# First feed-forward of a four-stage fused block: the last six weight chunks rounded by VectorE alone, and three pieces of work put elsewhere in their engines' orders

## What is computed

```python
wq = w.astype(jnp.float8_e4m3fn).astype(x.dtype)
y = jnp.einsum('bsi,io->bso', x, wq)
return y * scale

gate = jax.nn.silu(_quantized_matmul(x, gate_w, gate_scale))
up = _quantized_matmul(x, up_w, up_scale)
return _quantized_matmul(gate * up, down_w, down_scale)
```

## Time and profile before

| | us |
|---|---|
| Median of 3 runs (723.23 to 723.35) | 723.33 |
| The profiled execution's own time | 722.73 |
| Its span, first to last instruction | 720.9 |
| PE busy / DVE busy | 660.1 / 548.9 |
| ACT busy / POOL busy | 479.7 / 436.0 |

### The profile page before, as it was taken

How to read it: one execution, slowest core, us unless ns; L and a number is a source line. 1 busy time by engine, 2 the same in 40 slices (tenths; PEclk the granted TensorE clock), 3 DMA queues, 4 the chain that set the end, 5 groups by cost and what they waited for, 6 DMA issues and landing times.

```text
span 720.9 us, 16231 instructions
## 1 busy us (share of the span) xinstructions
PE 660.1 (92%) x5782; PEld 527.8 (73%) x5782; DVE 548.9 (76%) x1180; ACT 479.7 (67%) x982; POOL 436.0 (60%) x618
## 2 busy tenths in 40 slices
PE   2789999988899999999999999999999999999784
PEld 1567777667788877888888888888888888876442
DVE  3699999999787877676777676676767766766887
ACT  1577877756466576666666666666666666658994
POOL 2378878878877545565656656665656554464500
PEclk9999999999999999999999999999999999999997
DMA  8200003203201000000000100000100000000001
GB/s 282 77 9 9 10 9 117 70 1 106 86 1 38 15 1 2 15 30 9 23 24 17 28 9 25 23 16 16 31 9 16 15 1 3 1 1 1 31 29 60
DMA packets 26019, 22.83 MB, mean 32 GB/s; under 512 B 5041, under 2 KB 24402, under 8 KB 25810
## 3 DMA queue, kind: packets, MB, share of 16 engines
q1 hardware_dynamic: 24160, 20.92, 9.2%
q10 hardware_dynamic: 1778, 0.86, 0.4%
HBM read 19.67 MB, written 2.10 MB: 30 GB/s over the span
## 4 chain that ended last, share of the span: by engine, by line
POOL 38%; issue 26%; PE 15%; DVE 14%; ACT 3%; ACTq 1%; POOLq 1%; DVEq 0%
POOL rstd L734 14%; POOL pr L702 5%; POOL p_n L709 5%; PE banks L1594 2%; POOL w L725 2%; POOL w_raw L722 2%; PE banks L1613 2%; PE banks L1614 2%; DVE h_sum L1093 2%; DVE hid_b L1086 2%; POOL var L732 1%; POOL qk_norm L644 1%; DVE h_magic_b L1091 1%; DVE half L852 1%; POOL hid_lo L671 1%
## 5 line engine op out<-in xcount | busy, mean ns | idle before, releaser
L734 POOL TENSOR_TENSOR rstd<-var,minus_half 128x8 f32<-128x8 f32 x64 | 106.1, 1657 | 5.0
L709 POOL TENSOR_TENSOR p_n<-pr,pinv 128x256 f32<-128x256 f32 x64 | 39.3, 614 | 75.7 <-DVE pinv L1001 75.7
L702 POOL TENSOR_TENSOR pr<-pr,rstd 128x256 f32<-128x256 f32 x63 | 38.6, 613 | 74.1 <-DVE pr L1011 74.0
L1316 ACT ACTIVATE kT<-banks,gk_q 128x512 f32<-128x512 f32 x64 | 44.0, 688 | 49.1 <-PE banks L1755 49.1
L1745 PE MATMUL banks<-m_hi,z_hi 128*128 128x256 f32 x256 | 74.9, 293 | 0.7 <-DVE z_lo L992 0.6
L1745 PE MATMUL banks<-m_hi,z_lo 128*128 128x256 f32 x256 | 72.3, 283 | 0.0
L1745 PE MATMUL banks<-m_lo,z_hi 128*128 128x256 f32 x256 | 72.3, 282 | 0.0
L992 DVE TENSOR_TENSOR z_lo<-banks,z_hi 128x512 fp32r<-128x512 f32 x64 | 43.9, 686 | 29.1 <-ACT z_hi L1301 29.0
L1039 DVE TENSOR_REDUCE sums<-q_sq 128x4 f32<-128x512 f32 x64 | 43.7, 683 | 25.2 <-ACT q_sq L1340 25.2
L1362 ACT ACTIVATE qT<-banks 128x512 f32<-128x512 f32 x64 | 38.2, 597 | 32.9 <-PE banks L1849 32.9
L1007 DVE TENSOR_REDUCE pmax<-banks 128x4 f32<-128x256 f32 x64 | 27.0, 422 | 41.1 <-PE banks L1776 41.0
(11 more groups left out here) (194 smaller groups left out, 2059.2 us busy)
## 6 DMA issues: line engine op xcount, KB each, us to landing
w_raw<-in_L_xattn_Wq SPq DMA_DIRECT2D x4, 512.0 KB, 5.8
wo_raw<-in_L_xattn_Wo SPq DMA_DIRECT2D x1, 2048.0 KB, 9.2
k_ctx<-in_ctx SPq DMA_DIRECT2D x16, 128.0 KB, 2.7
w_raw<-in_L_ffn_w_gating SPq DMA_DIRECT2D x16, 128.0 KB, 2.3
out_x<-x_sb SPq DMA_DIRECT2D x4, 512.0 KB, 2.9
x_sb<-in_x SPq DMA_DIRECT2D x1, 1536.0 KB, 9.3
a_ctx<-in_ctx SPq DMA_DIRECT2D x16, 64.0 KB, 1.8
w_raw<-in_L_xattn_Wk SPq DMA_DIRECT2D x2, 512.0 KB, 9.1
```

The lines of the kernel that those rows point to most:

```text
L702: pool.tensor_tensor(pr[:, u % 2, :, :], pr[:, u % 2, :, :], roots_of[:, HC:2 * HC].unsqueeze(2).to_broadcast([P, HC, S]), ALU.mult).then_ ...
L709: pool.tensor_tensor(p_n[:, u % 2, :, :], pr[:, u % 2, :, :], pinv[:, u % 2, :].unsqueeze(2).to_broadcast([P, HC, S]), ALU.mult).then_inc( ...
L734: pool.tensor_tensor(rstd1[:, par, :], var1[:, :], minus_half[:, :].to_broadcast([P, 2 * HC]), ALU.pow).then_inc(root1, 1)
L1316: act.activation(kT[u % 2][:, :, :].rearrange("p h n -> p (h n)"), bank[2][:, :], ACT.Copy, scale=gk_q[:, :]).then_inc(kT_ready, 1)
```

## The change

The first late chunk is now chunk 12 instead of chunk 13. A new function rounds a chunk wholly on VectorE, and it stands where the late chunks' `w0_magic` stood, one place later each: chunk 12 after `rows_updated(NT - 2)`, chunk 13 in the step u = 2, and so on to chunk 17 in the step u = 6. GpSimd rounds chunks 0 to 11 only. On VectorE the four `normal` of tiles 4 to 7 move from between `hidden(0)` and `hidden(1)` to the step u = 2, behind `rows_updated(NT - 1)` and ahead of chunk 13, and `rows_updated(NT - 2)` now stands ahead of chunk 12's rounding. On GpSimd `weights_lo(23)` comes behind `hidden_lo(23)`.

```diff
-W0_LATE = W0_CHUNKS - 5
+W0_LATE = W0_CHUNKS - 6
...
+        def w0_rounded_here(dve, n):
+
+            w0_magic(dve, n)
+            dve.wait_ge(magic_steps, 2 * n + 2)
+            dve.wait_ge(w0_steps, 2 * n)
+            dve.tensor_tensor(w0_raw[:, w0_part(n)], w0_raw[:, w0_part(n)], rnd[:, n % 2, :], ALU.add).then_inc(w0_steps, 1)
+            dve.wait_ge(w0_steps, 2 * n + 1)
+            dve.tensor_tensor(w0[:, w0_part(n)], w0_raw[:, w0_part(n)], rnd[:, n % 2, :], ALU.subtract).then_inc(w0_steps, 1)
...
             probabilities0(NT - 1)
-            w0_rounded(pool, 12)
             rows_biased(NT - 1)
             hidden_lo(0)
             weights_lo(0)
             hidden_lo(1)
-            w0_rounded(pool, W0_LATE)
             weights_lo(1)
...
-                weights_lo(u)
+                if u < NG * J0 - 1:
+                    weights_lo(u)
                 hidden_lo(u)
-                if u <= W0_CHUNKS - W0_LATE:
-                    w0_rounded(pool, W0_LATE + u - 1)
             run_groups(J0, step, 2)
+            weights_lo(NG * J0 - 1)
...
             w0_magic(dve, 11)
-            w0_magic(dve, 12)
             exponential_sums0(NT - 1)
             hidden(0)
-            for r in range(GT, 2 * GT):
-                normal(r, f_xhat, f_xhat_ready, fT_done)
             hidden(1)
-            w0_magic(dve, W0_LATE)
             rows_updated(NT - 2)
+            w0_rounded_here(dve, W0_LATE)
...
                 hidden(u)
                 if u == 2:
                     rows_updated(NT - 1)
+                    for r in range(GT, 2 * GT):
+                        normal(r, f_xhat, f_xhat_ready, fT_done)
...
                 if u <= W0_CHUNKS - W0_LATE:
-                    w0_magic(dve, W0_LATE + u - 1)
+                    w0_rounded_here(dve, W0_LATE + u - 1)
```

## The result

The changed kernel takes 728.08 us (727.32 to 728.71, 6 runs), the kernel before 723.34 (722.45 to 725.38, 6 runs): a ratio of 1.0066 (95% interval 1.0054 to 1.0078), 4.7 us slower. The forecast was 2.5 us slower, 725.8 with a range up to 728.0. The direction and the places were right, the size was not. The two profiled executions lie further apart than the medians: 728.71 us, the slowest of its six, against 722.73.

What follows compares the result with a forecast made beforehand. TensorE was taken to bound the stage, except at its start, where group 0's down products wait for GpSimd's rounding. Profiled 722.73 + 3.2 (later products) - 0.7 (stage end) = 725.2, median 0.6 higher: 725.8 us, range 724.3 to 728.0.

Steps and rivals of the forecast that it cites:

- The replay: Group 0, chunk by chunk: 6.7 us of new TensorE waiting less 3.5 removed, chunk 17's product 3.2 us later.
- the two holds behind the long waits: GpSimd low halves hold chunk 13's second magic step (to 177.41) and chunk 17's subtraction (to 193.8).
- The tail: Stage end: the last low half no longer stands behind 0.74 us of next-stage weights, -0.7 us.
- the term for the clock: Rival, 20%: TensorE's clock halves after standing still 175.6 to 178.4, costing 0.8 to 1.7 us; a second fall up to 728.5.
- The rival that the holds fall away: Group 0: VectorE mostly not held by GpSimd, chunk 17's product 0.36 us earlier than before, time 722.2, no change; 11%.
- the last subtraction: Chunk 17: if only this VectorE instruction escapes GpSimd's low half, its product starts at 192.9, time 724.7.
- GpSimd's relief: Rival, 4%: VectorE delivers every chunk by its due time, all 3.5 us and the 0.7 come back: 719.1.

Runs made afterwards that it cites:

- both waits filled: The changed kernel with 11 unread matmuls before the second down product and 8 before chunk 17's, in TensorE's two long waits: 725.37 us, ratio 1.0034.
- the mended version: The changed kernel with normalisations of tiles 4 to 7 back, chunk 17 right behind hidden(6), those of tiles 8 to 11 behind group_scaled(0): 721.48 us, ratio 0.9970.
- chunk 13 first: The changed kernel with chunk 13 rounded ahead of the four normalisations in the step u = 2: 726.69 us, ratio 1.0053.
- chunk 17 first: The changed kernel with chunk 17 rounded ahead of the four normalisations of tiles 8 to 11 in the step u = 6: 726.0 us, ratio 1.0047.
- the first filled: The changed kernel with 11 unread matmuls in TensorE's first long wait only, ahead of the second down product: 726.1 us, ratio 1.0039.

## Why the prediction was wrong

- **The replay held.** Product 1 was forecast at 178.45 - 173.96 = 4.49 us after product 0: 4.47. Product 5, at 193.94 - 173.96 = 19.98: 20.07 with the clock kept up. The releasers were the ones named, and the two holds behind the long waits too: magic step at chunk 13, subtraction at chunk 17, with the 0.15 and about 0.3 us behind GpSimd's end that the earlier trace rows gave. At chunk 16 the replay held both magic steps. The rows of the kernel after have the first one free and the second and the addition held, with the same two remainders, and with the clock up the chunk was done when the replay had it (14.57 us after product 0 against 188.56 - 173.96 = 14.60):

```profile
187.60 0.28 DVE L467 TENSOR_SCALAR rnd<-w_raw 128x256 uint32<-128x256 uint32 x1
187.91 1.27 DVE L469 TENSOR_SCALAR rnd<-rnd 128x256 f32<-128x256 f32 x1
189.22 0.85 DVE L430 TENSOR_TENSOR w_raw<-w_raw,rnd 128x256 f32<-128x256 f32 x1
...
187.64 1.39 POOL L680 TENSOR_TENSOR hid_lo<-hid,hid_hi 128x512 fp32r<-128x512 f32 x1
189.00 0.78 POOL L673 TENSOR_TENSOR w_lo<-w_raw,w_hi 128x256 fp32r<-128x256 f32 x1
```

- **The tail held**: 0.74 us, with -0.7 taken.
- **What failed is the term for the clock.** The prediction put a fall "in the new gap" beside the forecast as a rival with 20%, for 0.8 to 1.7 us, and allowed a second one only as an end of it. The profiled execution had two, one behind each of the two long waits, 1.57 us each and 3.0 together, and filling the waits took the ratio from 1.0066 to 1.0034, 2.3 us. A term that belonged into the sum stood outside it; its price was right (1.57 lies within 0.8 to 1.7), its chance was too low and the second fall, in the gap of chunk 17, was missing from the sum. The evidence was read too weakly: the earlier trace rows showed a fall behind 0.65 of 2 us busy, and the replay itself had TensorE at next to nothing for 2.9 us. I set against it the 7.86 of 10 us of the earlier trace rows, a mean over a stretch with several short waits, which says nothing of one long one. And I looked at one gap where my own working had two, of 2.9 and 2.4 us.
- **It was not bad luck of one trace.** The mean granted clock of the six executions of the changed kernel lay between 0.982 and 0.987, with a median of 0.983; of the eight with both waits filled, between 0.984 and 0.990, with a median of 0.9885. How many falls each of them had in this stage is not known: only one execution of each kernel has a trace.
- **The rival that the holds fall away** was wrong: holds came at chunks 13, 15, 16 and 17, and the last subtraction did not escape. What the Trainium skill (VectorE: DVE Perf Modes, The DRAIN you can't avoid) says, that a semaphore costs nothing extra, by which the sum would have been up to 1.4 us smaller, found no support: an instruction that waits for the one ahead of it starts 0.03 to 0.04 us after its end (176.21 + 0.29 = 176.50, next at 176.53), one without a wait 0.08 before it (174.92 + 1.37 = 176.29, next at 176.21), and product 5 came no earlier than the replay had it. No run took a semaphore away alone.
- **GpSimd's relief was real**, and the mended version gains by it, by its order and by the tail: product 4, which waited longest before, comes 0.9 us earlier there than in the kernel before (12.33 against 13.20), though product 1 comes 0.7 later.

## What to carry to other kernels

Taking work off a full engine pays only if the engine that gets it does it ahead of what it feeds next: here the same rounding on VectorE, with the same tail, came out 4.7 us slower in one order and 2.2 (0.3%) faster in another. When a change opens waits like these on TensorE (2.3 to 2.6 us), put a stretch at half clock behind each into the sum (behind five of the seven such waits in these traces the clock fell: all three ahead of product 1 or its transposes, two of four ahead of product 5), and test by filling the wait with matmuls that nobody reads. Replay an in-order engine with what is queued behind each moved piece: the wait that vanished at chunk 17 came back one product later because of it.

## What the runs showed of the hardware

A fall of the clock to its lower level, where TensorE is the bound, cost 1.57 us twice in the kernel after. Read the same way, the falls with chunk 13 first cost 1.58 and 1.55, and the one with chunk 17 first 1.44 (4.75 from product 1 to 2, against 3.31); there the clock had fallen some 0.2 us before TensorE went back to work. Falls come in some executions and not in others: over the same work ahead of this stage, at 152 to 154 us, the granted clock is 0.50 in the trace with both waits filled and 1.00 in the one with the first filled. In one set of 25 executions of the kernel before the mean clocks lay from 0.984 to 0.993; the four at 0.984 took 723.9 to 724.5 us and the five at 0.993 about 722.4 to 722.6, though the slowest and the fastest of the set (725.84 and 721.7) had 0.985 and 0.989. That scatter is as large as the differences that this study looks for, so starts of products in the traces told more than the times. Dead matmuls can be worth their room: 19 of them took a kernel from 1.0066 to 1.0034 of the one before.
